# The last pair of a fused adapter kernel on one core: VectorE turns u, product 3 is split around the mixing, and four of the final stores change place or queue

## The reference

```python
# first layer: 8 experts of rank 16, the two best of each token
base = einsum('btd,od->bto', x, W)
logits = einsum('btd,ed->bte', x, Wr) + one_hot(language) * 5.0
topw, topi = top_k(logits, 2);  gates = scatter(softmax(topw), topi)
h = einsum('btd,erd->bter', x, A)
y = base + 2.0 * einsum('bter,bte,eor->bto', h, gates, B)
# second layer: 4 experts of rank 8, all of them, with a softmax gate
base_out = einsum('bsi,oi->bso', y, Wf) + bf
gates = softmax(einsum('bsi,ei->bse', y, Wrf))
out = x + base_out + einsum('bse,bseo->bso', gates * 2.0, Bm(Af(y)))
```

## Time and profile before

| | us |
|---|---|
| time, median of 3 runs (lowest to highest) | 324.01 (323.56 to 324.32) |
| the profiled execution, its own time | 323.14 |
| its span, first to last instruction | 321.8 |
| PE busy | 317.9 (99%) |
| DVE busy | 263.1 (82%) |
| ACT busy | 128.5 (40%) |
| last matmul of pair 7 ends | 318.94 |

### The profile page before, as it was taken

How to read it: one execution, slowest core, us unless ns; L and a number is a source line. 1 busy time by engine, 2 the same in 40 slices (tenths; PEclk the granted TensorE clock), 3 DMA queues, 4 the chain that set the end, 5 groups by cost and what they waited for, 6 DMA issues and landing times.

```text
span 321.8 us, 5997 instructions
## 1 busy us (share of the span) xinstructions
PE 317.9 (99%) x2245; PEld 311.7 (97%) x2245; DVE 263.1 (82%) x613; ACT 128.5 (40%) x258; POOL 1.4 (0%) x11
## 2 busy tenths in 40 slices
PE   8999999999999999999999999999999999999996
PEld 5999999999998999899999999999999999999996
DVE  5989999898799778988868968878895997788543
ACT  4962836495148236225412503421251250333110
POOL 1000000000000000000000000000000000000000
PEclk9999999999999999999999999999999999999999
DMA  7997000000000411700330150061025016003003
GB/s 289 417 403 272 2 2 0 2 0 2 0 2 0 132 30 40 261 2 0 115 149 1 64 197 0 0 199 62 0 73 188 0 32 229 0 0 125 10 0 132
DMA packets 10706, 27.60 MB, mean 86 GB/s; under 512 B 3166, under 2 KB 4702, under 8 KB 10688
## 3 DMA queue, kind: packets, MB, share of 16 engines
q1 hardware_dynamic: 10256, 26.83, 23.5%
q10 hardware_dynamic: 432, 0.53, 0.5%
HBM read 18.97 MB, written 8.39 MB: 85 GB/s over the span
## 4 chain that ended last, share of the span: by engine, by line
PE 98%; DMA 1%; DVE 0%; issue 0%
PE sums L1308 98%; DMA in<-part 1%; PE sums L1555 0%; DVE rows L1065 0%; DVE b_high L798 0%
## 5 line engine op out<-in xcount | busy, mean ns | idle before, releaser
L1308 PE MATMUL sums<-b_high,a_high 128*128 128x256 f32 (+1 forms) x224 | 45.5, 286 | 0.2 <-DVE b_high L798 0.2
L1308 PE MATMUL sums<-b_low,a_high 128*128 128x256 f32 (+1 forms) x224 | 45.4, 286 | 0.0
L1308 PE MATMUL sums<-b_high,a_low 128*128 128x256 f32 (+1 forms) x224 | 45.3, 286 | 0.0
L1308 PEld LDWEIGHTS sums<-b_high,a_high 128*128 128x128 f32 x224 | 34.7, 189 | 1.2 <-ACT a_high L541 1.1
L1308 PEld LDWEIGHTS sums<-b_low,a_high 128*128 128x128 f32 x224 | 34.7, 189 | 0.0
L1308 PEld LDWEIGHTS sums<-b_high,a_low 128*128 128x128 f32 x224 | 34.7, 188 | 0.0
L1308 PE MATMUL sums<-t_high,s_high 128*128 128x354 f32 x96 | 31.2, 325 | 0.0
L1308 PE MATMUL sums<-t_low,s_high 128*128 128x354 f32 x96 | 31.1, 324 | 0.0
L1308 PE MATMUL sums<-t_high,s_low 128*128 128x354 f32 x96 | 31.1, 324 | 0.0
L1065 DVE TENSOR_TENSOR rows<-sums,rows 128x354 f32<-128x354 f32 x48 | 24.4, 522 | 4.1 <-PE sums L1308 3.5
L1308 PE MATMUL sums<-ct_high,st_high 128*128 128x244 f32 (+1 forms) x80 | 25.6, 320 | 0.0
(11 more groups left out here) (152 smaller groups left out, 836.8 us busy)
## 6 DMA issues: line engine op xcount, KB each, us to landing
stage<-tokens SPq DMA_DIRECT2D x14, 512.0 KB, 4.0
out<-rows SPq DMA_DIRECT2D x14, 512.0 KB, 4.9
in<-part SPq DMA_DIRECT2D x7, 585.0 KB, 7.4
in<-part SPq DMA_DIRECT2D x4, 777.0 KB, 15.1
in<-part SPq DMA_DIRECT2D x4, 265.0 KB, 17.8
rows<-tokens SPq DMA_DIRECT2D x2, 512.0 KB, 13.4
out<-rows SPq DMA_DIRECT2D x3, 192.0 KB, 2.3
c_plain<-gate_proj SPq DMA_DIRECT2D x1, 544.0 KB, 19.3
```

The lines of the kernel that those rows point to most:

```text
L1308: return nc.tensor.matmul(out_, lhs, rhs, start=start, stop=stop, skip_group_check=True)
```

## The change

It does five things.

1. In pair 7 VectorE turns u as in pairs 2 to 6, in place of TensorE's two transposes; ScalarE and VectorE round and split it in halves. `u3_read` and `r22_read`, two additions into `rows`, stand ahead of v's chain, as in pairs 2 to 6, and product 5 ahead of small_y.
2. In pair 7 product 3 is cut in two: its first 6 matmuls stand ahead of the mixing (the tails, then A, D and B), its last 6 behind it. lora B stands ahead of the mixing too.
3. In all pairs ScalarE's copy of v from which VectorE subtracts comes first and increments `v_rounded`; the other one follows and increments a new semaphore, `v_again`, for which TensorE waits ahead of the tails' mixing beside `vt_ready`.
4. In pair 7 T1 is issued by ScalarE, behind A, and no longer by SyncE.
5. In the weight part the sums that were made in one instruction of several blocks are made one block at a time.

The diff, cut to its core:

```diff
         act: in pair(j)
-                if steady and not last:
+                if steady:
                     act.wait_ge(u_half_turned, j - 1)
                     copy(half_of(ut_high, 0), ut_plain_half(0)).then_inc(ut_half_high, 1)
                 act.wait_ge(u_turned, j + 1)
...
                 act.wait_ge(v_turned, j + 1)
-                copy(vt[2 * ER2:3 * ER2, :, :], vt_plain[0:ER2, :, :])
                 copy(vt[0:ER2, :, :], vt_plain[0:ER2, :, :]).then_inc(v_rounded, 1)
+
+                copy(vt[2 * ER2:3 * ER2, :, :], vt_plain[0:ER2, :, :]).then_inc(v_again, 1)
...
             act.dma_start(out[(TILES - 2) * P:(TILES - 1) * P, stored_at(0)], rows[:, 0, stored_at(0)])\
                 .then_inc(stored_a, 16)
+
+            act.dma_start(z_of(out[(TILES - 1) * P:TILES * P, :], STORED, HZ), z_of(rows[:, 1, :], STORED, HZ))\
+                .then_inc(stored_a, 16)
         dve: the weight part (make_s4, make_t2, make_t3, make_t4 alike)
-            def make_s3():
-
-                dve.wait_ge(f_s1, HALF)
-                minus(s3, a11, a21).then_inc(f_s3, HALF)
+            def make_s3(k):
+
+                dve.wait_ge(f_s1, k + 1)
+                minus(s3[:, k, :], a11[:, k, :], a21[:, k, :]).then_inc(f_s3, 1)
         dve: in pair(j)
-                if turning:
+                if steady:
+
                     turn_u(j)
...
-                if turning:
+                if steady:
                     add_u3()
                     add_r22()
...
-                if last:
-                    add_u3()
...
-                if last:
-                    add_r22()
         pe: in pair(j)
-                if last:
-                    turn_u()
...
-                if turning:
+                if steady:
                     product_5(j)
-                if steady:
                     small_y()
                 lora(BANK_A, 0, 0)
-                if second or last:
+                if second:
                     product_5(j)
...
-                if turning:
-                    lora(BANK_B, 1, 0)
-                    product_3(j)
-                    mixed_tails(j)
-                elif last:
-                    mixed_tails(j)
-                    lora(BANK_B, 1, 0)
-                else:
-                    lora(BANK_B, 1, 0)
-                    mixed_tails(j)
+                lora(BANK_B, 1, 0)
+                if last:
+
+                    product_3(j, range(HALF // 2))
+                elif steady:
+                    product_3(j).then_inc(p3_done, 1)
+                mixed_tails(j)
                 mixed(BANK_A, 0, 0).then_inc(a_done, 1)
                 mixed(BANK_D, 1, 1).then_inc(d_done, 1)
                 mixed(BANK_B, 1, 0).then_inc(b_done, 1)
-                if not turning:
-                    product_3(j)
+                if last:
+                    product_3(j, range(HALF // 2, HALF)).then_inc(p3_done, 1)
+                elif not steady:
+                    product_3(j).then_inc(p3_done, 1)
                 lora(BANK_C, 0, 1)
                 mixed(BANK_C, 0, 1).then_inc(c_done, 1)
```

More of the change, by code:

```diff
@@ L837, in make_s2, with make_s4, make_t2, make_t3 @@
                 minus(s2[:, k, :], s1[:, k, :], a11[:, k, :]).then_inc(f_s2, 1)
[L839 to L848, removed]
[L850 to L862 removed]
+            def make_s4(k):
+                dve.wait_ge(f_s2, k + 1)
+                minus(s4[:, k, :], a12[:, k, :], s2[:, k, :]).then_inc(f_s4, 1)
+            def make_t2(k):
+                dve.wait_ge(here_4[k], 16)
+                dve.wait_ge(f_t1, k + 1)
+                minus(t2[:, k, :], b22[:, k, :], t1[:, k, :]).then_inc(f_t2, 1)
+            def make_s3(k):
+                dve.wait_ge(f_s1, k + 1)
+                minus(s3[:, k, :], a11[:, k, :], a21[:, k, :]).then_inc(f_s3, 1)
+            def make_t3(k):
+                dve.wait_ge(here_4[k], 16)
+                dve.wait_ge(f_t1, k + 1)
+                minus(t3[:, k, :], b22[:, k, :], b12[:, k, :]).then_inc(f_t3, 1)
+            def make_t4(k):
+                dve.wait_ge(f_t2, k + 1)
+                minus(t4[:, k, :], b21[:, k, :], t2[:, k, :]).then_inc(f_t4, 1)
             def add_out(q, c, lower, onto):
@@ L949, in vector_program @@
             make_s2(3)
-            make_s4(1, 3)
+            for k in range(1, HALF):
+                make_s4(k)
             make_t2(0)
@@ L961, in vector_program @@
             split_step(12)
-            make_t2(2, 2)
+            make_t2(2)
+            make_t2(3)
             split_step(13)
-            make_s3()
+            for k in range(HALF):
+                make_s3(k)
             dve.wait_ge(gate_high, 1)
@@ L981, in vector_program @@
             split_step(15)
-            make_t3()
+            for k in range(HALF):
+                make_t3(k)
             dve.wait_ge(lang_here, 16)
@@ L997, in vector_program @@
             split_step(16)
-            make_t4()
+            for k in range(HALF):
+                make_t4(k)
             for n in range(17, 20):
@@ L1082, in pair @@
                 steady = not first and not second
-                turning = steady and not last
                 base = STEPS * j + VEC_START
@@ L1233, in pair @@
                                         negate=True).then_inc(neg_max_ready, 1)
-                if second or turning:
+                if not first:
                     next_s(S4)
@@ L1252, in pair @@
                 ins.then_inc(v_turned, 1)
-                if turning:
+                if steady and not last:
                     split_s(j + 1, S2)
-                if last:
-                    add_r22()
                 dve.wait_ge(v_rounded, j + 1)
@@ L1415, in tail, with wide @@
                 return last
-            def wide(n, a_high, a_low, a_at, b_high, b_low, fresh):
-                for k in range(HALF):
+            def wide(n, a_high, a_low, a_at, b_high, b_low, fresh, chunks=range(HALF)):
+                for k in chunks:
                     for kind in (HH, HL, LH):
@@ L1502, in narrow_products, with product_3 @@
                 narrow_of_s(BANK_NC, S4, cn_high[B22], cn_low[B22], False).then_inc(p3n_done, 1)
-            def product_3(j):
+            def product_3(j, chunks=range(HALF)):
                 pe.wait_ge(s_split, 4 * j + 4)
                 pe.wait_ge(r22_read, j + 1)
-                of_s(BANK_C, S4, cw_high[B22], cw_low[B22], False).then_inc(p3_done, 1)
+                return of_s(BANK_C, S4, cw_high[B22], cw_low[B22], False, chunks)
             def pair(j, first=False, second=False, last=False):
                 steady = not first and not second
-                turning = steady and not last
                 s_no = S_NO_FIRST if first else S_NO
```

22 lines of the change are left out of this document (10 added, 12 removed).

## The result

The changed kernel takes 324.31 us (median of 22 runs, 323.57 to 324.82), the kernel before 323.85 us (22 runs, 323.21 to 324.65). The ratio is 1.0015, with a 95% interval of 1.0010 to 1.0021: 0.5 us slower (0.3 to 0.7), and just inside the 0.2% that was set as the bound of no change. The forecast was 324.8 with a range of 323.8 to 325.2.

A forecast was written before the change was run, and what follows sets the result against it. TensorE's work, then what follows its last matmul, bounds the kernel; after the change the last stores' drain sets the end. The median 324.01 + 0.81 gives 324.8, with TensorE's -0.22 off the path; range 323.8 to 325.2.

The forecast's parts named there:

- the drain: Pair 7's last stores: 3.13 us of DMA work from 318.78 sets the end, +0.81 us; chance 0.70.
- TensorE, -0.22: Pair 7: TensorE's two transposes of u go, -0.22 us of its work, no longer on the path to the end.
- u's chain, slack 0.31: Pair 7: u turned on VectorE, `ut_low` whole at 310.42, small_y at 310.73; 0.31 us of slack, no wait.
- v's chain, slack 0.34, and 0.08 of wait without part 3: Pair 7: v ready at 315.81, tails' mixing at 316.15; 0.34 us of slack, with old copies a 0.08 us wait.
- The tails +1.25: Pair 7: the tails' mixing moves from 314.90 to 316.15, +1.25 us, and their addition and stores with it.
- The order of issue: Last stores: T1 on ScalarE lets SyncE issue C at 319.30, just when ready; left on SyncE, 319.96, 0.66 us later.
- my lower bound: Last stores: with C's 0.82 us from issue to first data, data start at 318.30 and end at 321.43, +0.33.
- What follows the last byte: End of the kernel: data end (321.10 before) and span end (321.8 before) were both moved by the same +0.81 us.
- The weight part, "nothing": Weight part: sums made block by block add work on VectorE that TensorE doesn't see, so no cost in time.
- Its cover: Weight part: VectorE has split operands four steps ahead, some 3.4 us each; TensorE must be 10 us faster to see it.
- My 2.4 us: Weight part: at most +0.47 us on VectorE for each of five splits of four-block sums, 2.4 us in all.
- A new wait on TensorE: Pair 7, rival: u's or v's chain late, TensorE stops ahead of small_y or the tails, 325.1 to 325.3; chance 0.11.

The follow-up runs named there:

- old_copies: The changed kernel with ScalarE's two copies of v in their old order (part 3 undone): +0.6 us (0.4 to 0.9) against the kernel before.
- t1_on_sync: The changed kernel with T1 issued by SyncE behind T0 (part 4 undone): +0.6 us (0.3 to 1.0) against the kernel before.
- old_sums: The changed kernel with the weight part of the kernel before (part 5 undone): +0.4 us (0.1 to 0.8) against the kernel before.
- sums_only: The kernel before with part 5 alone, weight sums one block at a time: +0.7 us (0.4 to 1.1) against the kernel before.
- shorter_end: The changed kernel with old weight sums, five merged last stores and pair 7's tails added per tile: 0.0 us (-0.3 to 0.3) against the kernel before.
- c_halves: shorter_end with C added and stored in two halves of 192 columns: +0.3 us (-0.1 to 0.5) against the kernel before.
- split_only: The kernel before with part 2 alone, lora B and half of product 3 ahead of the mixing: +1.5 us (1.0 to 1.9).

## Why the prediction was right, and where it was off

The measured time lies in the range, and the forecast case, the drain, is the one that the runs show. The size was off by nearly half: +0.81 us forecast, +0.46 measured between the medians. The forecast put 0.57 on slower and 0.39 on no change, and no change within 0.2% is what came.

- **TensorE, -0.22:** right, -0.26, and not on the path, as said.
- **u's chain, slack 0.31:** right, 0.40. Its addition and transposes overlap a little more than I had let them.
- **v's chain, slack 0.34, and 0.08 of wait without part 3:** right in kind, 0.30, and 0.29 of wait in the last matmul's start. A late semaphore costs more than the lateness, since the next weight load starts late too (old_copies).
- **The tails +1.25:** right, +1.20.
- **The order of issue:** C's issue came at 319.88, 0.11 us behind its addition. Left on SyncE, T1 held C's issue back by 0.61 us, as I had it (0.66), and the end by 0.08: the work of the engines decides (t1_on_sync).
- **The drain, +0.81: the term that was mis-sized.** Its work was right (3.13 forecast, 3.07 measured). Its start was not: I took T0's 1.30 us from issue to first data; A, issued 0.06 us behind T0, had its data 0.88 us after its issue, near the 0.82 us of C's row of before, my lower bound. From product 7's start data began at 11.54 where 11.95 was forecast, took 3.22 us for 3.13, and ended at 14.76: +0.50 for +0.81.
- **What follows the last byte:** I took it as constant, 0.73 us. It is 0.51 in the changed kernel: the sixteenth share of C, which lands 0.27 us behind the others before, is not late there. +0.50 - 0.22 is the +0.28 of the table.
- **The weight part, "nothing": this step failed.** Its cover held: VectorE was busy 0.5 to 1.0 us longer in the first 109 us with part 5 (99.08 in the changed kernel for 98.12 in old_sums, 98.95 in sums_only for 98.42 before), and TensorE didn't wait. My 2.4 us took five sums of four blocks; they are of 3, 2, 4, 4 and 4. But the cost came by another way: 0.18 us in pair 2, where a pause of VectorE in a chain with 0.26 us of slack came with 12 more of its instructions ahead of the loop. Why it pauses stays open.
- **A new wait on TensorE:** none in pair 7, but the lateness of pair 2 is of that kind, u's chain at small_y, in a place where I had not looked for it.

0.28 at the end and 0.18 in pair 2 make 0.46 us, the difference of the medians, though the interval (0.3 to 0.7) would allow for other sums too. The two errors, 0.53 us too much at the end and 0.18 too little in the loop, partly cancelled. The forecast of +0.81 stood beyond the bound of 0.65 us, and so most of the chance on slower; with C's row for the start, which was the nearer one, it would have been +0.33 and on the other side.

## What to carry to other kernels

When one engine is busy for 99% of the span, ask first what the last bytes wait for: work moved ahead of the point at which the stores can leave delays them, and 0.26 us off the busy engine is worth nothing once the DMA engines are still draining behind it. Price the last stores by their work on all 16 engines, and take the time from issue to first byte from the fastest row as well as the slowest. An edit far from the critical path can still cost something elsewhere, here with 12 more instructions ahead of a loop: compare the first pass of each loop, and the instruction queues in the last microseconds, before and after.

## What the hardware showed that was not expected

- When one packet of 8192 bytes of code (0.35 to 0.69 us long) fell into the last stores or right behind them, the sixteenth share of C landed 0.27 us (before), 0.46 (shorter_end), 0.48 (c_halves), 0.52 (sums_only) and 0.86 us (split_only) behind the fifteenth. In the changed kernel, with the packet 9.4 us ahead of the end of C's data, the sixteen land within 0.21 us.
- VectorE stood for 0.18 us with nothing to wait for, at the same instruction of the loop's first pass in seven profiles of kernels with part 5, and in none of the seven others.
- Two stores issued within 0.06 us by two engines: the one of 128 pieces had its first data after 0.88 us, the one of 256 pieces after 1.47, behind the first one's. Alone in front, the one of 256 pieces took 1.30 us before.
